# Routed FFN: the rows of a block are gathered five blocks ahead instead of four, in the same three buffers

## The reference, cut to what matters

```python
scores = jax.nn.sigmoid(x @ gate_w.T) + bias          # 16 experts
topk_w, topk_idx = jax.lax.top_k(scores, 4)
topk_w = topk_w / (jnp.sum(topk_w, axis=-1, keepdims=True) + 1e-20)
cw = jnp.sum(one_hot(topk_idx, 16) * topk_w[..., None], axis=1)
g = jnp.einsum('th,eih->eti', x, Wg)                  # inner width 256
u = jnp.einsum('th,eih->eti', x, Wu)
out = jnp.einsum('eti,ehi->th', silu(g) * u * cw.T[:, :, None], Wd)
out = out + silu(x @ Sg.T) * (x @ Su.T) @ Sd.T        # one shared expert
```

## Time and profile before

| | us |
|---|---|
| median of 3 runs | 2701.8 (2691.83 to 2703.66) |
| profiled execution, its own time | 2701.01 |
| its span, first to last instruction | 2699.3 |
| its block loops (first turn to last scatter) | 1684.2 to 1948.8 and 2409.8 to 2675.7 |

### The profile page before, as it was taken

The page is one execution under the profiler, slowest core; times in us unless marked ns, Lnnn a source line. Parts: engine busy times, 40 slices in busy tenths (PEclk is TensorE's granted clock), DMA queues, the critical chain, the costliest instruction groups (busy, mean ns, idle before and its releaser), DMA issues. The chain is left out here.

```text
span 2699.3 us, 42041 instructions
## 1 busy us (share of the span) xinstructions
PE 2518.7 (93%) x14382; PEld 1749.3 (65%) x14382; DVE 1919.5 (71%) x3640; ACT 1496.0 (55%) x2530; POOL 874.1 (32%) x818
## 2 busy tenths in 40 slices
PE   7899999989999999999999988899868999898996
PEld 5444446768888888888888875566544444465663
DVE  6888634568777777777777677677678887376775
ACT  4778822335555555555555542566447778325663
POOL 2100214255435343434435220355411001014553
PEclk9899999989999999999999998999988999899998
DMA  4000000010000000000000006888820000268888
GB/s 179 1 1 1 1 21 1 1 52 20 21 25 21 20 28 17 24 17 24 17 24 23 15 1 233 272 195 203 188 94 1 1 1 2 78 216 258 200 198 212
DMA packets 68719, 196.23 MB, mean 73 GB/s; under 512 B 8960, under 2 KB 9728, under 8 KB 63392
## 3 DMA queue, kind: packets, MB, share of 16 engines
q1 hardware_dynamic: 47456, 144.25, 15.9%
q0 software_dynamic: 21056, 49.30, 9.9%
HBM read 153.14 MB, written 40.37 MB: 72 GB/s over the span
## 5 line engine op out<-in xcount | busy, mean ns | idle before, releaser
L1510 ACT ACTIVATE L1a_ph<-single 128x512 fp32r<-128x512 f32 (+3 forms) x384 | 174.3, 489 | 182.0 <-PE single L1595 181.3
L1501 ACT ACTIVATE L1a_probs<-pair,L1a_least 128x128 f32<-128x128 f32 (+7 forms) x256 | 189.9, 744 | 73.4 <-DVE L1a_least L1646 72.3
L1652 DVE TENSOR_TENSOR L1a_pl<-single,L1a_ph 128x512 fp32r<-128x512 f32 (+3 forms) x384 | 199.5, 549 | 42.3 <-ACT L1a_ph L1510 41.7
L1668 DVE SCALAR_TENSOR_TENSOR x<-single,L1a_rinv,x 128x512 f32<-128x512 f32 x256 | 189.5, 745 | 56.1 <-PE single L1251 55.8
L1478 POOL TENSOR_TENSOR L1a_swapped<-L1a_swapped,L1a_sin 128x512 f32<-128x512 f32 x80 | 129.3, 1617 | 296.2 <-ACT L1a_swapped L1542 296.2
L1646 DVE TENSOR_REDUCE L1a_least<-pair 128x1 f32<-128x128 f32 (+7 forms) x256 | 190.7, 750 | 42.9 <-PE pair L1584 42.3
L538 ACT ACTIVATE L0a_probsT<-pair 128x896 f32<-128x896 f32 (+2 forms) x192 | 148.9, 811 | 55.9 <-PE pair L677 44.1
L538 ACT ACTIVATE L1b_probsT<-pair 128x896 f32<-128x896 f32 (+2 forms) x192 | 148.9, 811 | 54.9 <-PE pair L677 43.0
L837 DVE CUSTOM_DVE_ANT_0 single<-single,later 128x384 f32<-128x384 f32 (+1 forms) x256 | 155.4, 646 | 20.6 <-PE single L654 20.2
L1595 PE MATMUL single<-ident,L1a_probs 128*128 128x128 f32 x1152 | 169.0, 274 | 0.8 <-DVE L1a_pl L1652 0.4
L1249 PE MATMUL single<-L1a_xh,L1a_wh 128*128 128x512 f32 x384 | 159.2, 415 | 0.0
(11 more groups left out here) (545 smaller groups left out, 7061.2 us busy)
## 6 DMA issues: line engine op xcount, KB each, us to landing
L1f_wd<-in_L1f_w SPq DMA_DIRECT2D x48, 512.0 KB
L1g_wd<-in_L1f_w SPq DMA_DIRECT2D x48, 512.0 KB
L1a_raw<-in_L1a_w SPq DMA_DIRECT2D x80, 256.0 KB, 2.6
L1f_store<-in_L1f_w SPq DMA_DIRECT2D x16, 1024.0 KB, 9.0
L1g_store<-in_L1f_w SPq DMA_DIRECT2D x16, 1024.0 KB, 9.8
sum<-L0a_pad_row SPq DMA_DIRECT2D x2, 2304.0 KB, 17.2
sum<-x SPq DMA_DIRECT2D x16, 256.0 KB
x<-sum SPq DMA_DIRECT2D x16, 256.0 KB, 6.3
```

Of the source, the lines that this page charges most:

```text
L1501: act.activation(probs[:, u % 2, 0:n], g.pair[u % 2][:, 0:n], ACT.Exp, bias=least[:, u % 4:u % 4 + 1], scale=-1.0, accum_out=rsum[:, h % 2 ...
L1510: act.activation(p_tile(ph, u, i), turned_bank(u, i), ACT.Copy).then_inc(p_high, 1)
L1652: dve.tensor_tensor(p_tile(pl, u, i), turned_bank(u, i), p_tile(ph, u, i).bitcast(F32), ALU.subtract)\
L1668: dve.scalar_tensor_tensor(out=g.x[:, t, :], in0=aux_bank(("O", h, t)), scalar=rinv[:, h % 2, t:t + 1], in1=g.x[:, t, :], op0=ALU.mult, op ...
```

## The change

`AHEAD` goes from 4 to 5. `XRING`, the number of row buffers, stays 3.

```diff
-XRING, YRING, PAIRS, AHEAD, EARLY = 3, 3, 3, 4, 3
+XRING, YRING, PAIRS, AHEAD, EARLY = 3, 3, 3, 5, 3
```

## The result

| | before | after |
|---|---|---|
| median, us | 2702.73 (4 runs, 2691.83 to 2711.87) | 2667.16 (4 runs, 2663.75 to 2668.32) |
| profiled execution, us | 2701.01 | 2663.75 |
| its span, us | 2699.3 | 2662.0 |

The ratio is 0.9868 with a 95% interval of 0.983 to 0.9906, so 35.6 us or 1.3% less, with 0.9% to 1.7% as bounds. The forecast was 2674.

What follows compares the result with a forecast made beforehand. PE's waits for late gathers were taken to cost up to 37.9 us in the block loops. Gains of 20 (early) and 8 us (calm) off 2701.0 gave 2673, put at 2674 for the median; range 2662 to 2694.

Steps and rivals of the forecast that it cites:

- What bounds the kernel: Block loops of L1f and L1g: PE waits for late gathers; scatter spacing gives at most 37.9 us to gain.
- The new wait in POOL's order costs 0: POOL's loop: the earlier gather's wait for block b + 2 to be turned is already over, costing 0.
- The calm part, 8 us: Scatter 11 to 42, both stages: a 9.9 us lead covers the flights; 8 us gained, bounds 4 and 9.8.
- The early part, 20 us: Scatter 0 to 11, while SP loads experts into store: 20 of 28.2 us gained, 4 us a stage left.
- nothing left: Bound for scatter 0 to 11: no stall remains there, so the gain is 28.2 us.
- all of it comes back: Rival: every PE stall goes, as DMA engines take the load; gain 36 to 38 us, 2665; chance 0.16.
- The wait changes its name: Rival: early on, down weights queued behind store loads come as late as the gather; 2688 to 2694; chance 0.20.
- It does nothing: Rival: gathers issued sooner only stand longer in POOL's queue and land as now; 2700; chance 0.06.
- the scatters set the pace: Rival: slower, as scatter b waits for scatter b - 2 and landings take longer; about 2716; chance 0.06.
- What would show it: Signs: gather waits under 10 us, clock near 1.00, scatter 0 to 11 about 60.5 us, 11 to 42 about 160.

## Why the prediction was right, and where its size was off

**What bounds the kernel.** Right. The spacing of the scatters gave 37.9 us as the most that could come back, and 36.4 did. The flight of the gather against its lead explains four and five ahead with one formula, and three ahead once its 5.45 us are stretched by the low clock. One reading was too strong: a gather of the calm part doesn't as a rule outlast 4.8 us. The prediction had one flight of 5.78 us from the chain; in the changed kernel the median there is 4.5, and only the longer ones stalled. (Scatter 42 also isn't the last with a turn in its iteration, that is scatter 43; as both kernels are measured up to the same scatter, nothing hangs on it.)

**The new wait in POOL's order costs 0.** Right: in the loop POOL loses nothing to `b_turned`; its two real waits for a turn lie before scatter 0, where it waited for the first y anyway (8.9 us before, 6.1 us after).

**The calm part, 8 us.** Right in kind, a bit low: 9.2 of 9.8.

**The early part, 20 us.** This is the term that was mis-sized: 27.3 came back, not 20. The step that failed is that the DMA engines, being nearly full, fall behind by 2.1 us in each group, so that 4 us a stage stay. It took the DMA share times the window as an amount of work, 17.5 us for 5.2 MB, that stays the same however the transfers lie. In the changed kernel a group's 15.4 us moved 289 to 359 GB/s, that is 4.5 to 5.5 MB, with no stall, and without the eight loads it was no faster. From scatter 0 to 11 of L1f the engines moved 17.7 MB in both kernels. Before, that was a share of 0.88 over 70.7 us, 62.2 us; after, 1.01 over 57.1 us, 57.6. So the same bytes took less engine time, and a share of 1 was no limit. Of its bounds, "nothing left (DMA engines do the same work quicker when they are never empty)", which the prediction named and didn't take, is what happened. The share depends on what is moved and on how much at once. The changed kernel in L1f by queue (q1 the loads from SP, q0 gathers and scatters; packets, MB, share), first scatter 0 to 11, then 11 to 42:

```profile
q1 hardware_dynamic: 2445, 12.04, 56.3%
q0 software_dynamic: 2425, 5.66, 44.1%
...
q0 software_dynamic: 6902, 16.11, 57.2%
q1 hardware_dynamic: 4465, 16.26, 31.6%
```

A MB of rows costs 4.4 us of share in the early part and 5.6 in the calm one, a MB of loads 2.7 and 3.1. So the calm part reads 0.88 at only 200 GB/s, since half of its bytes are rows and each MB reads dearer. The real ceiling over 15 us and more lies near 365 GB/s (single stretches of 4 or 5 us reach 386 to 399): with 256 or 512 KB more in an iteration the rate stops at 361 to 368, and time is lost, 4 and 19 us. The group needs 5.2 MB, 14.4 us at 365 GB/s, which is under 15.4, so the engines can follow. It is close: the longest gather used 9.3 of its 9.9 us.

**The Trainium skill.** The prediction set the limit of about 358 GB/s in "DMA: Bandwidth & Descriptors", section "Specifications", against the trace and let the trace decide. The windows it took were too long for that, since they average over full and slack stretches. Cut into 4 us, the trace of before shows a full one beside a slack one:

```profile
1710.00:1714.00 4.00, 2.13 (x6) 1.58 (x7) 1.75 (x3) 0.60 (x1) 0.80 (x1) 0.71 1.04 386
1714.00:1718.00 4.00, 4.00 (x15) 2.45 (x14) 1.14 (x3) 1.62 (x3) 1.12 (x1) 0.87 0.68 173
```

386 GB/s at a share of 1.04, then 173 at 0.68: the engines caught up while PE stood still and had little to do after it. The runs show 359 to 368 GB/s in full stretches of 15 to 27 us, within 3% of the figure, and the rival "all of it comes back", priced at 2665, was nearly right. Whether it is HBM that sets this rate no run here shows.

**The other rivals.** "The wait changes its name" names the right next customer, the down weights, but with five ahead it didn't come true: PE waits for them only with added load, or with six ahead, and there for 1.5 us in all. "It does nothing" and "the scatters set the pace" didn't occur; scatter b's wait for scatter b - 2 reached 3.6 us at POOL with six ahead, and DVE had no wait for a scatter.

**What would show it.** Waits for gathers went to none, the clock to 1.00, 0 to 11 to 57 us (60.5 was said), 11 to 42 to 159 (160 said), DMA share over 0.95: all as said but for the size of the early part.

## What to carry to other kernels

Find for every prefetch the time from its issue to its use and compare it with its flight under load, not its flight in quiet; here one more block ahead cost no buffer, since the buffer had been free a period before anybody filled it. Don't take a DMA engine's busy share for an amount of work: judge by GB/s in a stretch that is full, against what is needed in a period. And when a stall goes, count the clock too, here about a third of the early excess of one stage, by one run.

## What was unexpected of the hardware

- The DMA share goes over 1 (1.05 at 359 and at 368 GB/s) and stands at 0.88 at 200 GB/s, so it doesn't measure headroom. A MB of gathers and scatters reads nearly twice as dear as a MB of plain loads (5.6 against 3.1 us in the calm part).
- An idle of PE of 2.3 to 2.5 us is followed by the low clock in some places (`down` 3.03 us after 2.33, and 3.65 after 2.46, granted clock 0.72 from 1733 to 1739 us) and not in others (1.95 us after 2.54 us of idle, granted clock 1.00 from 1721 to 1724).
- With the gather instead of the scatter first at POOL, ACT started its next operation 0.65 us later in every other block, though nothing joins the two in the program. The order cost 10 to 11 us a stage, and its cause is open.
